# The weighted sum of four gathered neighbours on VectorE in the last stage of a graph layer

## What is computed

```python
def _lap_mul(A, x):
    d = 1.0 / jnp.sqrt(jnp.sum(A, axis=-1))
    return d[:, None] * (A @ (d[:, None] * x))
z = leaky_relu(_lap_mul(A, x) @ W1 + b1, 0.1)
d2 = maximum(sq[:, None] + sq[None, :] - 2.0 * (z @ z.T), 0.0)   # sq = row sums of z * z
S = exp(-sqrt(d2 + 1e-10) / 2)
S = where(rank of S in its row < 4, S, 0.0)                      # the four nearest nodes
A2 = S + A
x = layernorm(x + (_lap_mul(A2, x) @ W2 + b2))
```

## Time and profile before

| | us |
|---|---|
| three timed runs, median | 2692.11 |
| lowest and highest of the three | 2690.73, 2692.74 |
| span of the profiled execution | 2759.5 |
| PE busy, share of the span | 2482.6, 90% |
| DVE busy | 2319.8, 84% |
| ACT busy | 1606.7, 58% |
| POOL busy | 1195.4, 43% |

### The profile page before, as it was taken

The page is one execution under the profiler, slowest core; times in us unless marked ns, Lnnn a source line. Parts: engine busy times, 40 slices in busy tenths (PEclk is TensorE's granted clock), DMA queues, the critical chain, the costliest instruction groups (busy, mean ns, idle before and its releaser), DMA issues.

```text
span 2759.5 us, 29107 instructions
## 1 busy us (share of the span) xinstructions
PE 2482.6 (90%) x9356; PEld 1722.4 (62%) x9356; DVE 2319.8 (84%) x1411; ACT 1606.7 (58%) x1905; POOL 1195.4 (43%) x987
## 2 busy tenths in 40 slices
PE   1367999999999998899999999999999987888978
PEld 0133444444677776578787877778787764666655
DVE  7998899977788888999999999999999773666766
ACT  0000000000477767999989899899988763555655
POOL 0000000000000000377778878788878956666760
PEclk9688999999999999999999999999999988999989
DMA  9999999995899960146555655555655688988975
GB/s 385 421 402 408 398 421 421 421 421 215 320 349 342 338 226 7 35 141 183 151 163 138 179 142 175 140 170 149 174 143 167 182 309 343 347 324 320 345 295 208
DMA packets 147949, 718.58 MB, mean 260 GB/s; under 512 B 19025, under 2 KB 26961, under 8 KB 86609
## 3 DMA queue, kind: packets, MB, share of 16 engines
q1 hardware_dynamic: 124384, 670.49, 65.6%
q0 software_dynamic: 18800, 37.77, 5.7%
q10 hardware_dynamic: 4608, 8.39, 0.8%
HBM read 680.40 MB, written 36.18 MB: 260 GB/s over the span
## 4 chain that ended last, share of the span: by engine, by line
PE 56%; issue 10%; ACT 10%; DVE 9%; DMA 7%; POOL 3%; another core or an unknown queue 3%; SPq 0%; ACTq 0%; POOLq 0%; DVEq 0%
PE PS L767 17%; PE PS L866 5%; PE PS L868 5%; PE PS L867 5%; DMA ring<-at 4%; ACT R L1141 3%; PE PS L834 3%; PE PS L910 3%; PE PS L921 3%; PE PS L911 3%; PE PS L830 2%; PE PS L831 2%; ACT ah_t L1191 2%; DVE R L1621 2%
## 5 line engine op out<-in xcount | busy, mean ns | idle before, releaser
L1299 POOL TENSOR_TENSOR al<-ring,ah 128x1024 fp32r<-128x1024 f32 x264 | 644.0, 2441 | 180.5 <-ACT ah L1112 168.7
L1621 DVE MAX8 R<-R 128x8 f32<-128x8192 f32 x64 | 555.9, 8685 | 68.1 <-ACT R L1141 67.9
L1141 ACT ACTIVATE R<-PS 128x1024 f32<-128x1024 f32 x512 | 518.1, 1018 | 114.1 <-PE PS L874 83.1
L1624 DVE FIND_INDEX8 R<-R,R 128x8 uint32<-128x8192 f32 x64 | 555.9, 8685 | 0.3 <-issue 0.3
L1272 POOL CAST zst<-zh 128x128 fp32r<-128x128 f32 (+1 forms) x64 | 26.2, 410 | 1113.2 <-DVE zl L1556 811.5
L866 PE MATMUL PS<-zh,zst 128*128 128x512 f32 x1024 | 407.3, 398 | 28.6 <-ACT PS L1127 12.7
L868 PE MATMUL PS<-zh,zst 128*128 128x512 f32 x1024 | 400.4, 391 | 0.0
L867 PE MATMUL PS<-zl,zst 128*128 128x512 f32 x1024 | 400.1, 391 | 0.0
L1456 POOL DMA_INDIRECT R<-xs_dram,R x256 | 279.7, 1093 | 145.2 <-issue 75.5
L1127 ACT ACTIVATE PS<-R 128x1024 f32<-128x1024 f32 x310 | 318.0, 1026 | 6.6
L1046 ACT ACTIVATE tiny<-rowsum 128x4 f32<-128x4 f32 x16 | 3.3, 205 | 481.2 <-DVE rowsum L1491 481.2
(11 more groups left out here) (177 smaller groups left out, 4469.9 us busy)
## 6 DMA issues: line engine op xcount, KB each, us to landing
R<-at SPq DMA_DIRECT2D x152, 1024.0 KB, 13.3
ring<-at SPq DMA_DIRECT2D x148, 1024.0 KB, 9.5
ring<-at SPq DMA_DIRECT2D x264, 512.0 KB, 3.9
cache<-at SPq DMA_DIRECT2D x117, 1024.0 KB, 20.2
raw_sq<-at SPq DMA_DIRECT2D x21, 1024.0 KB
raw_z<-at SPq DMA_DIRECT2D x20, 1024.0 KB
raw_ring<-at SPq DMA_DIRECT2D x20, 1024.0 KB
acc_dram<-R POOLq DMA_DIRECT2D x78, 256.0 KB, 5.7
```

The lines of the kernel that those rows point to most:

```text
L1141: act.activation(score[j % 2][:, c * EC:(c + 1) * EC].rearrange("p (b c) -> p b c", b=2), pair(first, j, c), ACT.Copy).then_inc(copied, 1)
L1299: pool.tensor_tensor(al[:, k % SPLIT], raw[k % RAW], ah[:, k % SPLIT].bitcast(F32), ALU.subtract)\
L1621: v.max(top[:, j], score[j % 2]).then_inc(dve3, 1)
L1624: v.max_index(place[:, j], top[:, j], score[j % 2]).then_inc(placed, 1)
```

## The change

ACT's function `weigh` goes, with its semaphore `wt_ok` and its wait for `placed`. DVE's function `neighbours` waits for the gathers itself and forms the weighted sum of the four rows by one multiplication and three multiply-and-add operations of 128x128, each scaled by one column of `sval` and each but the last in place in the gathered rows; the last writes `gs`. The operations are linked one by one. They stand at the same places of DVE's order as the two additions did. The gathers, their number and their buffers stay as they are.

```diff
--- before.py
+++ after.py
@@ -395,7 +395,6 @@
         prod_t = sem("prod_t")
         light_ok = sem("light_ok")
         s_gx = [[sem(f"s_gx{k}_{j}") for j in range(TB)] for k in range(2)]
-        wt_ok = sem("wt_ok")
         gs_ok = sem("gs_ok")
         u_ok = sem("u_ok")
         yf_light = sem("yf_light")
@@ -1195,13 +1194,6 @@
                     act.wait_ge(out_ok, f - 1)
                 act.dma_start(xb[f % 2], x[:, FIN[f] * TB:(FIN[f] + 1) * TB]).then_inc(s_xb[f % 2], 16)
 
-            def weigh(f, j):
-                act.wait_ge(s_gx[f % 2][j], 16 * KNN * (f // 2 + 1))
-                t = FIN[f] * TB + j
-                for m in range(KNN):
-                    i = act.activation(gx[f % 2][:, j, m], gx[f % 2][:, j, m], ACT.Copy, scale=sval[:, t, m:m + 1])
-                i.then_inc(wt_ok, 1)
-
             def heavy_y(f):
                 act.wait_ge(u_ok, f + 1)
                 if f >= 2:
@@ -1241,12 +1233,9 @@
                     s_of_distances(G - 1)
                 if u == BY_POOL + 1:
                     root_of_sums(G - 1)
-                    act.wait_ge(placed, T)
                 for f in range(B):
                     if u == FIN_AT[f] - 3:
                         load_xb(f)
-                    if 0 <= u - FIN_AT[f] + 7 < TB:
-                        weigh(f, u - FIN_AT[f] + 7)
                     if u == FIN_AT[f] + 1 and FIN[f] in HEAVIES:
                         heavy_y(f)
                     if u == FIN_AT[f] + 6:
@@ -1675,11 +1664,17 @@
                 v.tensor_tensor(cols, cols, PS[:, 2 + b % 2], ALU.add).then_inc(light_ok, 1)
 
             def neighbours(f, j):
-                v.wait_ge(wt_ok, TB * f + j + 1)
-                lt(v.tensor_tensor(gx[f % 2][:, j, 0:2], gx[f % 2][:, j, 0:2], gx[f % 2][:, j, 2:4], ALU.add))
+                t = FIN[f] * TB + j
+                rows = gx[f % 2][:, j]
+                v.wait_ge(s_gx[f % 2][j], 16 * KNN * (f // 2 + 1))
+                lt(v.tensor_scalar(rows[:, 0], rows[:, 0], sval[:, t, 0:1], None, ALU.mult))
+                for m in range(1, KNN - 1):
+                    lt(v.scalar_tensor_tensor(rows[:, m], rows[:, m], sval[:, t, m:m + 1], rows[:, m - 1],
+                                              ALU.mult, ALU.add))
                 if f >= 2:
                     v.wait_ge(u_ok, f - 1)
-                v.tensor_tensor(gs[f % 2][:, j], gx[f % 2][:, j, 0], gx[f % 2][:, j, 1], ALU.add).then_inc(gs_ok, 1)
+                v.scalar_tensor_tensor(gs[f % 2][:, j], rows[:, KNN - 1], sval[:, t, KNN - 1:KNN], rows[:, KNN - 2],
+                                       ALU.mult, ALU.add).then_inc(gs_ok, 1)
 
             def light_y(f):
                 v.wait_ge(u_ok, f + 1)
```

## The result

The changed kernel takes 2703.8 us (median of five runs, 2701.1 to 2707.7), the kernel before 2692.7 in the same series (2690.7 to 2696.1): ratio 1.0039, interval 1.0028 to 1.0050. It is 11 us slower. The forecast of no change failed; the slow rival, +12.4, has the sign and the size. The range of 2681 to 2708 holds the time, and only by that rival.

The account below looks back on a forecast made before the run. In the last stage no engine is full, PE nearest (busy 415 of 495 us). ACT's relief -7.7, late rows +2.8 and bunching +5.2 sum to +0.3 us: timed 2692.4 us, range 2681 to 2708.

Parts of the forecast that it names:

- The forecast of no change: Whole kernel: terms sum to +0.3 us, timed 2692.4 us, within 0.2% of today; chance 0.45.
- the slow rival: Last stage, rows 13 to 15: DVE becomes the bound, +12.4 us, or 2704.5; chance 0.22.
- The price of a tile: DVE, last stage: one multiplication and three multiply-and-adds take 1.34 us a tile, against 0.66 today.
- ACT's part, -7.7: Last stage: without ACT's weighing, PE's waits for roundings right behind a weighing give back 7.7 us.
- The seven waits: Seven places where PE idled for a rounding right behind a weighing: 8.8 us together, 7.7 capped at 1.17 a tile.
- In rows 9 to 12 I take nothing: Block rows 9 to 12: DVE's longer tiles cost nothing, since plain products or loads leave room.
- PE still covers it: Block rows 10 to 12: PE's 50.1 us a row exceed DVE's 48.2 after the change.
- 2.8 + 5.2 us in rows 13 to 15: Late rows: 2.8 us where DVE becomes the fuller engine, 5.2 from bunched tiles, 0.7 in each of 7.4 blocks.
- the forecast's own range: Whole kernel, by the low and the high price of a tile: 2688 to 2698 us.
- The rival "DVE becomes the bound": Rows 13 to 15: none of the added 20.1 us is regained, ACT's 7.7 come off, +12.4; chance 0.22.
- PE's waits for remainders beyond 15 us: Sign in the last stage: PE's waits for DVE's remainders (L1668) growing past 15 us mean DVE is the bound.
- The other edits at nothing: DVE's own gather wait, POOL's later gathers and the dropped `placed` wait were costed at nothing.

Follow-up runs that it names:

- run 3: Changed kernel's four DVE operations added to the kernel before, with ACT still weighing too, so both engines weigh: 2714.3 us, ratio 1.0070 to the kernel before.
- new profile of before: The kernel before, unedited, run and profiled once more: 2692.8 us, span 2690.9.
- the early half of the change alone: DVE weighs only the tiles of the first nine blocks finished, ACT the last seven as in the kernel before: 2699.4 us, ratio 1.0019.
- no weighing: Kernel before with the weighing left out on both engines, DVE doing its two additions and waiting for the gather itself: 2681.4 us, ratio 0.9950.
- experiment 4: Changed kernel with its multiplication replaced by a fourth multiply-and-add: 2706.7 us, ratio 1.0053 to the kernel before, against 1.0039 for the change.
- experiment 7: Kernel before, ACT still weighing, with weighings and additions moved by tables: 2688.9 us, ratio 0.9980; second table with later weighings 2688.1 us, 0.9972.

## Why the prediction was right and wrong

The time lay in the range and the chance of slower was 0.30, but the likeliest case was no change, and the rival that came out has its size by luck, as said below. By its steps:

- **The price of a tile**, 1.34 us: right (1.36 to 1.41), both operations within 35 ns of their figures.
- **ACT's part, -7.7**: right in sign, too small for the relief alone, which is worth 13.5 us (10 to 17); beside DVE's longer tile it gave 8 (from run 3 to the change). The seven waits of the earlier trace rows were taken one by one and capped at a tile each. Two more places in that trace, at 2461.63 and 2680.02, have a rounding right behind a weighing too, and PE idle before it for 4.97 and 13.31 us; with them the same sum is 10.0. In the new profile of before PE waits for the rounding 16 times, 18.8 us, and 7 times, 6.3 us, after. The step counted only roundings that stood right behind a weighing, and it counted them in an execution that had other stalls. Which of the further waits hang on a weighing some products back was not followed up.
- **"In rows 9 to 12 I take nothing"** and, under it, **"PE still covers it"**: this failed. Both weighing, the early rows cost 10.3 us; the early half of the change alone is 5 us slower. PE's waits for remainders rose by 3.9 us in the early rows and 6.4 in the late. The step added up each block row, 50.1 us of PE against 48.2 of DVE, and so let DVE use the four plain products of a row for work that stood elsewhere. DVE cannot: `wait_halves_free` holds a remainder until the split product two before is done, so DVE gets one split product ahead at most. The sum that decides is that of a few successive products. A split product leaves DVE 2.72 - 2.27 = 0.45 us; a tile was 0.21 over that before and is 0.9 over it now; four in a row make 3.6 us, with the residual (1.12) and the moments on top.
- **2.8 + 5.2 us in rows 13 to 15**: the mechanism was named, the size, 8.0, was too small; 11.7 were measured with both weighing, 12.8 from no weighing to the change. Half of a bunch's lateness was let go behind plain products, and only the part of three tiles above the idle time was counted. In the forecast's own range the bunches at the low price come to 3.0 by this rule, not 4.0; the 2688 there is right.
- **The rival "DVE becomes the bound"**, +12.4, came out in sign and size (+11), and its sign, PE's waits for remainders beyond 15 us, is there (19.8). But the size came out by luck: it put the whole cost, 20.1, into the late rows, where 11.7 to 12.8 fell, and left out as much in the early ones; over all rows the tile costs 19 to 24, and the 7.7 set against it measured 8 to 13.5. Nor is DVE the bound by its sum: with the tiles moved the same kernel beats both. What binds is DVE's order.
- **The other edits at nothing**: right. DVE never waited for a gather, POOL's wait for DVE grew from 1.5 to 9.7 us without showing in the end, and GpSimd held up nothing that mattered (experiment 4).

## What to carry to other kernels

When work moves to an engine that feeds another through two buffers, don't compare sums over a stage: compare what it must do between two successive hand-overs with the time that one of them lasts, and look at what already stands there. An idle engine (DVE, 84 of 454 us) can still be late, and the cure is to move the work to places where nothing is owed, before giving the idea up: one pattern for all blocks gave back the 11 us, a table for each block made it 6 and 10.7 us faster than before. Not all of this is the change's own: the kernel before gained 5 and 7.5 us by moved places too (experiment 7). And read a profile only after its span agrees with the timed runs; otherwise take another.

## What the runs showed of the hardware

Of POOL's gathers, some get longer beside DVE's remainders, and none beside its multiplications. Of the 256 of the changed kernel 31 took over 1.5 us: each began during one half of a remainder and ended 0.81 to 0.83 us after that half did. Of the 133 that began during a remainder 80 took under 1.1 us, and the 25 that began during a multiplication 0.94 to 1.02. In the stretch of row 11 shown above, POOL's timeline (start, duration):

```profile
2437.30 0.95 POOL L1445 DMA_INDIRECT R<-xs_dram,R  x1 [0.30 <-issue]
2438.55 0.99 POOL L1445 DMA_INDIRECT R<-xs_dram,R  x1 [0.30 <-issue]
2439.84 1.97 POOL L1445 DMA_INDIRECT R<-xs_dram,R  x1 [0.30 <-issue]
2442.11 0.95 POOL L1445 DMA_INDIRECT R<-xs_dram,R  x1 [0.30 <-issue]
2443.37 0.98 POOL L1445 DMA_INDIRECT R<-xs_dram,R  x1 [0.30 <-issue]
2444.65 1.97 POOL L1445 DMA_INDIRECT R<-xs_dram,R  x1 [0.30 <-issue]
```

The gathers that begin with a multiplication (2437.30, 2442.11) take the usual 0.95 us, and so nearly do the two that begin just before a remainder (2438.55, 2443.37). The two that begin as the second half of a remainder starts take 1.97, and both end 0.82 us after that remainder does (2440.99 and 2445.80). The page "SBUF — State Buffer" of the Trainium skill, section "Who interferes with whom", says that a VectorE operation with two inputs in SBUF is in the way of a GpSimd instruction that reads SBUF. A gather of this kernel reads its indices there, and these rows agree; but no run changes the number of inputs of a remainder, so that this is the reason is not shown. In the change it cost nothing that the runs show.
